# Which of several waits stands first: thirty places of an eight-layer kernel

## The reference

```python
x = x + spiking_attention(layernorm(x))   # 16 heads, q, k, v to spike means of 4 steps, softmax, projection
x = x + fp4_gated_ffn(layernorm(x))       # inputs and weights quantised in blocks of 16, silu(gate) * up, down
x = x + mamba4(layernorm(x))              # 4 layers; each: xz = x @ Wi.T; conv of 4 taps; u = silu(.);
                                          # dt = softplus(.); h_t = exp(dt_t*A)*h_(t-1) + dt_t*B_t*u_t;
                                          # y_t = C_t . h_t; (y + u*Dp) * silu(z) @ Wo.T
x = x + ternary_ffn(layernorm(x))
x = x + causal_linear_attention(layernorm(x))
x = x + top1_of_8_experts(layernorm(x))
x = x + long_convolution(layernorm(x))
x = x + dense_and_retrieved_experts(layernorm(x))   # top 8 of product keys, gathered up and down rows
```

## Time and profile before

| | |
|---|---|
| median of 3 runs | 1876.51 us (1872.69 to 1880.26) |
| profiled execution | 1873.34 us |
| its span | 1871.4 us, 27470 instructions |
| busy | PE 80%, PEld 57%, DVE 81%, ACT 71%, POOL 64% |
| granted TensorE clock, mean | 0.864 of full speed |
| DMA | 170.12 MB, mean 91 GB/s |

### The profile page before, as it was taken

One profiled execution on the slowest core, in us unless ns is written; L12 is line 12 of the kernel. 1 busy time (PEld: TensorE's weight loads), 2 busy tenths in 40 slices (PEclk: granted clock), 3 DMA queues, 4 the chain that ended last, 5 costly groups with the idle time before them and its releaser, 6 DMA issues.

```text
span 1871.4 us, 27470 instructions
## 1 busy us (share of the span) xinstructions
PE 1504.1 (80%) x9445; PEld 1072.7 (57%) x9445; DVE 1507.5 (81%) x2326; ACT 1324.6 (71%) x2672; POOL 1193.7 (64%) x999
## 2 busy tenths in 40 slices
PE   6777667567899988777788999878999887789976
PEld 3433334334577666544366776656666665667855
DVE  5688899999898799978998888898698998941254
ACT  4476656656897678777687877878688788754464
POOL 4158557666776568876765566878677778840046
PEclk7667777777999899878798999988799998899997
DMA  5032403423543433220343444331245542102300
GB/s 192 1 92 72 109 16 80 98 74 82 142 114 109 136 108 103 69 55 24 86 110 103 138 117 125 102 97 55 77 137 159 148 119 69 60 28 94 113 18 6
DMA packets 84586, 170.12 MB, mean 91 GB/s; under 512 B 9440, under 2 KB 14944, under 8 KB 84064
## 3 DMA queue, kind: packets, MB, share of 16 engines
q1 hardware_dynamic: 84448, 168.37, 32.7%
HBM read 99.13 MB, written 2.10 MB: 54 GB/s over the span
## 4 chain that ended last, share of the span: by engine, by line
PE 23%; DVE 16%; ACT 9%; POOL 7%; issue 5%; DMA 2%; SPq 1%; DVEq 0%; POOLq 0%; ACTq 0%
DVE m L1050 6%; DVE dtuB L1042 4%; PE ps L1473 3%; PE ps L1465 3%; ACT m L1026 3%; PE ps L1312 2%; PE ps L1180 2%; POOL o L1658 2%; POOL o L1653 2%; PE ps L965 2%; POOL m L1059 1%; PE ps L1756 1%; PE ps L1078 1%; ACT L347 1%; PE ps L1323 1%
## 5 line engine op out<-in xcount | busy, mean ns | idle before, releaser
L1059 POOL TENSOR_TENSOR m<-m 128x1024 f32<-128x1024 f32 x256 | 767.3, 3002 | 170.3 <-DVE m L1050 169.8
L1050 DVE TENSOR_TENSOR_SCAN m<-m,dtuB 128x1024 f32<-128x1024 f32 x256 | 584.4, 2283 | 31.5 <-PE ps L1078 10.0
L1026 ACT ACTIVATE m<-m,Aneg 128x255 f32<-128x255 f32 x1024 | 429.4, 496 | 26.7 <-DMA m<-m 18.5
L1042 DVE TENSOR_TENSOR dtuB<-m 128x1024 f32<-128x1024 f32 x256 | 374.7, 1464 | 13.1 <-DMA m<-m 6.2
L1465 PE MATMUL ps<-o 128*128 128x256 f32 x512 | 150.7, 406 | 19.8 <-DVE X L1409 11.8
L364 POOL TENSOR_TENSOR o<-o,mhalf 128x2 f32<-128x2 f32 x64 | 19.4, 304 | 222.2 <-DVE o L358 222.0
L1078 PE MATMUL ps<-m,w_const 128*32 128x256 f32 x2048 | 150.4, 425 | 7.4 <-POOL m L1059 7.3
L1432 ACT ACTIVATE o<-ps,w_mo 128x256 f32<-128x256 f32 x256 | 114.1, 472 | 59.7 <-PE ps L1465 58.0
L965 PE MATMUL ps<-m,wc 128*128 128x256 f32 x512 | 130.2, 411 | 10.9 <-ACT m L385 10.7
L1180 PE MATMUL ps<-o 128*128 128x256 f32 x512 | 127.2, 398 | 9.7 <-DVE o L1117 4.3
L1473 PE MATMUL ps<-o 128*128 128x128 f32 x1024 | 130.7, 281 | 3.2 <-ACT o L1432 3.1
(11 more groups left out here) (253 smaller groups left out, 2932.4 us busy)
## 6 DMA issues: line engine op xcount, KB each, us to landing
m<-m SPq DMA_DIRECT2D x256, 256.0 KB, 4.8
m<-spread SPq DMA_DIRECT2D x64, 512.0 KB, 4.9
o<-in_mox SPq DMA_DIRECT2D x128, 256.0 KB, 3.1
o<-in_l1x SPq DMA_DIRECT2D x88, 256.0 KB, 2.9
w_mb<-in_mb SPq DMA_DIRECT2D x1, 2290.0 KB, 12.1
m<-in_cwr SPq DMA_DIRECT2D x1, 2048.0 KB, 16.0
w_l3f<-in_l3f SPq DMA_DIRECT2D x1, 1536.0 KB, 17.6
X<-in_x SPq DMA_DIRECT2D x4, 256.0 KB, 6.6
```

The lines of the kernel that those rows point to most:

```text
L1026: op = e.activation(dA[at % NA][:, j, 1:CH], R[q][:, h * CH + 1:h * CH + CH], ACT.Exp, scale=Aneg[:, l, 4 * g + j:4 * g + j + 1])
L1042: e.tensor_tensor(dtuB[:, :, :], bc(R[q][:, (2 + h) * CH:(3 + h) * CH].unsqueeze(1), 4, CH), Br[k % 2], ALU.mult).then_inc(S.dve, n.tick(f ...
L1050: e.tensor_tensor_scan(flat(G[at % NG]), flat(dA[at % NA]), flat(dtuB[:, :, :]), 0.0, ALU.mult, ALU.add).then_inc(S.dve, n.tick(f"s{g}"))
L1059: e.tensor_tensor(G[at % NG], G[at % NG], Cr[k % 2], ALU.mult).then_inc(S.pool, n.tick(f"c{g}"))
```

## The change

The operations, their order on every engine and the set of waits ahead of each stay as they are (one exception of form: waits that stood ahead of a loop now stand ahead of its first instruction). In thirty places, over all stages, the waits ahead of an instruction are written in another sequence, so that another one stands first. The core of the diff; the places left out are of the same form (L0Attn, L0Ffn, L2Attn, L2Ffn, L3Attn and L3Ffn, most with a wait for a one-time load or a set-up value):

```diff
@@ -658,17 +658,17 @@
                 yield
+                e.wait_ge(T.pe, n.pe("qk"))
                 e.wait_ge(loaded["l0a"], 16)
-                e.wait_ge(T.pe, n.pe("qk"))
                 for i, name in enumerate(("q", "k")):
...
                 for h in range(16):
+                    e.wait_ge(T.pe, n.pe(f"s{h}"))
                     if h >= 4:
                         e.wait_ge(T.pe, n.pe(f"z{h // 4 - 1}{h % 4}"))
-                    e.wait_ge(T.pe, n.pe(f"s{h}"))
                     table(e, "exp")
@@ -683,8 +683,8 @@
                 yield
+                e.wait_ge(T.act, n.act("xT"))
                 e.wait_ge(loaded["l0a"], 16)
-                e.wait_ge(T.act, n.act("xT"))
                 for i, name in enumerate(("q", "k")):
@@ -696,8 +696,8 @@
                 def values(j):
+                    e.wait_ge(T.act, n.act(f"e{4 * j + 3}"))
                     e.wait_ge(T.pool, n.pool("vz3"))
-                    e.wait_ge(T.act, n.act(f"e{4 * j + 3}"))
                     for kt in range(2):
@@ -708,10 +708,10 @@
                     j, g = divmod(h, 4)
+                    if g == 0:
+                        e.wait_ge(T.dve, n.dve(f"m{j}"))
                     if h >= len(score):
                         e.wait_ge(T.act, n.act(f"e{h - len(score)}"))
-                    if g == 0:
-                        e.wait_ge(T.dve, n.dve(f"m{j}"))
                     for kt in range(2):
@@ -937,12 +937,13 @@
                 v, b = chains[k % 2], F.bank
+                if k >= 2:
+                    e.wait_ge(F.dve, n.dve("y"))
                 if k:
...
                     c, l = UNITS[k - 2]
-                    e.wait_ge(F.dve, n.dve("y"))
                     for i in range(2):
@@ -1016,11 +1017,11 @@
                     at, q, h = 8 * k + g, g % 4, g // 4
+                    if h == 0:
+                        e.wait_ge(*self.landed(n, q, 0))
                     if at >= NA:
...
                         e.wait_ge(S.dve, S.at(job, "dve", f"s{was}"))
-                    if h == 0:
-                        e.wait_ge(*self.landed(n, q, 0))
                     for j in range(4):
@@ -1028,34 +1029,36 @@
             def dve(self, e, n, k):
-                e.wait_ge(*self.spread(k, "B"))
-                if k == 0:
-                    e.wait_ge(U.pool, U.at(0, "pool", f"wc{NL - 1}"))
-                    for T in Os:
-                        e.wait_ge(T.act, T.at(0, "act", "e15"))
                 for g in range(8):
...
                         e.wait_ge(S.dve, n.dve(f"s{g - 1}") if g else S.at(k - 1, "dve", "s7"))
+                    if g == 0:
+                        e.wait_ge(*self.spread(k, "B"))
+                    if at == 0:
+                        e.wait_ge(U.pool, U.at(0, "pool", f"wc{NL - 1}"))
+                        for T in Os:
+                            e.wait_ge(T.act, T.at(0, "act", "e15"))
                     if h == 0:
...
                     yield
+                    e.wait_ge(S.dve, n.dve(f"b{g}"))
+                    e.wait_ge(S.act, n.act(f"a{g}"))
                     if at >= NG:
...
                         e.wait_ge(S.pe, S.at(job, "pe", f"y{was}"))
-                    e.wait_ge(S.act, n.act(f"a{g}"))
-                    e.wait_ge(S.dve, n.dve(f"b{g}"))
                     e.tensor_tensor_scan(flat(G[at % NG]), flat(dA[at % NA]), flat(dtuB[:, :, :]), 0.0, ALU.mult, ALU.add).then_inc(
...
             def pool(self, e, n, k):
-                e.wait_ge(*self.spread(k, "C"))
                 for g in range(8):
...
                     e.wait_ge(S.dve, n.dve(f"s{g}"))
+                    if g == 0:
+                        e.wait_ge(*self.spread(k, "C"))
                     e.tensor_tensor(G[at % NG], G[at % NG], Cr[k % 2], ALU.mult).then_inc(S.pool, n.tick(f"c{g}"))
@@ -1398,13 +1401,13 @@
                 yield
+                e.wait_ge(T.pe, n.pe("b2"))
                 e.wait_ge(T.act, n.act("xn1"))
-                e.wait_ge(T.pe, n.pe("b2"))
                 e.tensor_tensor(X2(c), ps2(self.bank(3)), X2(c), ALU.add).then_inc(T.dve, n.tick("b2"))
...
                 for x in range(8):
+                    e.wait_ge(T.pe, n.pe(f"y{x}"))
                     e.wait_ge(T.dve, n.dve(f"x{x - 1}1" if x else "b2"))
-                    e.wait_ge(T.pe, n.pe(f"y{x}"))
                     for i in range(2):
@@ -1426,9 +1429,9 @@
                     for k in range(4):
+                        e.wait_ge(T.pe, n.pe(f"h{x}{k}"))
                         if k == 0 and x >= 2:
                             e.wait_ge(T.pe, n.pe(f"y{x - 2}"))
-                        e.wait_ge(T.pe, n.pe(f"h{x}{k}"))
                         e.activation(v.hd[x % 2][:, k, :], self.bank(5 * x + 4 + k)[:, 0:CH], ACT.Relu,
@@ -1465,10 +1468,11 @@
                         yield
-                    e.wait_ge(*self.landed(n, 2 * x + 1))
                     for k in range(4):
...
                             e.wait_ge(T.act, n.act(f"h{x}{max(k, 2)}"))
+                        if k == 0:
+                            e.wait_ge(*self.landed(n, 2 * x + 1))
                         for i in range(2):
@@ -1610,11 +1614,15 @@
                     yield
-                    e.wait_ge(T.pe, n.pe(f"D{i}"))
                     for h in range(4):
-                        e.wait_ge(T.pool, n.pool(f"E{i}{h}"))
+                        if h % 2 == 0:
+                            e.wait_ge(T.pool, n.pool(f"E{i}{h}"))
                         if i or h:
                             e.wait_ge(T.pool, n.pool(f"w{i}{h - 1}" if h else f"w{i - 1}3"))
+                        if h % 2:
+                            e.wait_ge(T.pool, n.pool(f"E{i}{h}"))
+                        if h == 0:
+                            e.wait_ge(T.pe, n.pe(f"D{i}"))
                         e.scalar_tensor_tensor(v.md, v.Em[h % 2], v.s8[:, h, 7:8], o[:, :], ALU.is_ge, ALU.mult).then_inc(
@@ -1641,8 +1649,8 @@
                             e.tensor_tensor(v.e64, v.e64, bc(v.rinv.unsqueeze(2), 4, 64), ALU.mult).then_inc(T.pool, n.tick(f"r{i}"))
+                            e.wait_ge(T.pool, n.pool(f"r{i}"))
                             e.wait_ge(T.dve, n.dve(f"fl{i}"))
-                            e.wait_ge(T.pool, n.pool(f"r{i}"))
                             p4 = v.e64.rearrange("p h (a b) -> p (h a) b", b=8)
```

More of the change, by code:

```diff
@@ L645, in pool @@
                 yield
+                e.wait_ge(T.act, n.act("xn1"))
                 e.wait_ge(loaded["l0a"], 16)
-                e.wait_ge(T.act, n.act("xn1"))
                 e.tensor_tensor(X2(c), X2(c), row(w("l0a", "ob")), ALU.add).then_inc(T.pool, n.tick("ob"))
                 yield
+                e.wait_ge(T.dve, n.dve("u3"))
                 e.wait_ge(U.pool, U.at(0, "pool", T.name))
-                e.wait_ge(T.dve, n.dve("u3"))
                 spread_pool(e, n, T, v.va)
@@ L1316, in values @@
                 def values(j):
+                    e.wait_ge(T.act, n.act(f"p{2 * j + 1}"))
                     e.wait_ge(T.pool, n.pool("vz3"))
-                    e.wait_ge(T.act, n.act(f"p{2 * j + 1}"))
                     for i in range(2):
@@ L1384, in dve @@
                 yield from norm_dve(e, n, T, v, X2(c))
+                e.wait_ge(T.pe, n.pe("lg"))
                 e.wait_ge(loaded["mo"], 16)
                 e.wait_ge(loaded["const"], 16)
-                e.wait_ge(T.pe, n.pe("lg"))
                 e.tensor_tensor(v.lg, self.bank(1)[:, 0:16].rearrange("p (a b) -> p a b", a=2), bc(w("mo", "gb").unsqueeze(1), 2, 8),
@@ L1491, in dve @@
                 yield from norm_dve(e, n, T, v, X2(c))
+                e.wait_ge(T.act, n.act("xT"))
                 e.wait_ge(loaded["l3a"], 16)
                 e.wait_ge(U.dve, U.at(0, "dve", "r7"))
-                e.wait_ge(T.act, n.act("xT"))
                 e.tensor_tensor(v.xa, v.xT, Apow[:, :], ALU.mult).then_inc(T.dve, n.tick("xa"))
+                e.wait_ge(T.dve, n.dve("xa"))
                 e.wait_ge(U.pool, U.at(0, "pool", "onesF"))
-                e.wait_ge(T.dve, n.dve("xa"))
                 e.tensor_tensor_scan(v.sc, bc(onesF[:, 0:1], CH), v.xa, 0.0, ALU.mult, ALU.add).then_inc(T.dve, n.tick("s0"))
@@ L1504, in dve @@
                 yield
+                e.wait_ge(T.pe, n.pe("o"))
                 e.wait_ge(T.pool, n.pool("pb"))
-                e.wait_ge(T.pe, n.pe("o"))
                 e.tensor_tensor(v.r, ps2(T.banks[1]), v.xn, ALU.add).then_inc(T.dve, n.tick("r"))
@@ L1544, in pe @@
                 yield
+                e.wait_ge(T.act, n.act("gl"))
                 e.wait_ge(loaded["l3a"], 16)
-                e.wait_ge(T.act, n.act("gl"))
                 for i in range(2):
@@ L1749, in pe @@
                         yield
-                    e.wait_ge(T.dve, n.dve(f"x{i - 1}" if i else "d"))
                     for h in range(4):
                         e.wait_ge(T.act, n.act(f"w{i}{h}"))
+                        if h == 0:
+                            e.wait_ge(T.dve, n.dve(f"x{i - 1}" if i else "d"))
```

## The result

| | before | after |
|---|---|---|
| median of the runs, us | 1878.38 (1872.69 to 1881.46, 4 runs) | 1850.82 (1848.11 to 1857.45, 4 runs) |
| ratio, 95% interval | | 0.9862 (0.9824 to 0.9900) |
| profiled execution, us | 1873.34 | 1852.99 |
| its span, us, and granted clock | 1871.4, 0.864 | 1851.2, 0.863 |

The forecast was 1856.5 us, with a range from 1842 to 1873 and 0.74 on faster; the sum made for the profiled execution was 1853.3. So the total was right. The experiments show that its parts were not. The medians are 27.6 us apart; the ratio, which is one of means, makes it 26.

The account below looks back on a forecast made before the run. It held that no engine is saturated and hand-overs between instructions cost visible time. Latencies of 8 us and hand-overs between jobs of 12 took 1873.3 to 1853.3 us; the median, 3.2 above, was 1856.5, range 1842 to 1873.

Parts of the forecast that it names:

- What bounds it: Whole kernel: no engine saturated (DVE 81%, PE 80% busy); hand-overs a visible part, issue 97 us of the chain.
- The scan, 0.10 us a place: Scan L1050: its product's wait moves onto the instruction, saving 0.10 us at 27 chain pieces, 2.7 us from 681 us on.
- Other separate waits and PE, (1.9 + 1) x 1.57: Other late waits moved onto instructions: 31 chain pieces at 0.06 us save 1.9 us, PE's 1; scaled to the whole run.
- 0.6 x 1.57 against for the wrong-way ones: L716 and L673 now carry an early wait, the late one separate: 0.6 us lost on the chain, scaled by 1.57.
- The hand-over: Between scan jobs, DVE's product starts before POOL's at 11 places: 2.2 us less each on DVE, 1.04 more on POOL.
- take half of 24: Of DVE's 24 us saved at hand-overs between jobs, half reaches the end: 12 us, bounds 0 and 24.
- The sum, 8 + 12: Whole kernel: 8 us from wait latencies plus 12 from hand-overs, 1873.3 to 1853.3 us for the profiled execution.
- Only the latencies: Rival: L1042 shortens, but its gain becomes waiting for landings, or POOL still begins first; 1868.5 us, chance 0.22.
- POOL becomes the bound: Rival: POOL's longer last product delays L1078, L843 and the front; up to 24 us more, 1900 us, chance 0.04.
- The place of a wait costs nothing: Rival: the 0.12 us before the scan are DVE's own finish; time stays 1876.5 us, chance 0.04.
- Signs: Profile after: product-to-scan gap 0.04 us without wait piece, L1042 mean about 1370 ns, L1059 about 3047, issue under 90 us.

Follow-up runs that it names:

- e7: Changed kernel with L716's wrong-way waits turned back and six kinds of late separate wait written first: 1853.2 us, ratio to before 0.9848.
- e5: Kernel before with one satisfied wait written first at POOL's product of group 7, so POOL starts later: 1855.5 us, ratio 0.9884.
- e6: Changed kernel with a satisfied wait written first at group 4 of DVE's product ahead of the scan: 1891.7 us, ratio to before 1.0058.
- the place: The edit of DVE's product ahead of the scan: at group 0 the wait for the last scan rides on it; alone on the kernel before, 1850.1 us.
- e1: Changed kernel with B's landing written first again at group 0 of the product ahead of the scan: 1869.0 us, ratio to before 0.9933.
- e2: Kernel before with only the waits of the product ahead of the scan (L1042) in the new order: 1850.1 us, ratio 0.9846.
- e12: Changed kernel with POOL's product waiting for DVE's next product (groups 0 to 6) instead of the scan: 1855.2 us, ratio to before 0.9866.
- e3: Kernel before with only the scan's three waits (L1050) turned round: 1871.9 us, ratio 0.9956.
- e4: Kernel before with all of the change except the scan and the product ahead of it (28 places): 1869.9 us, ratio 0.9937.
- e8: Kernel before with both DVE edits of the scan stage, product and scan, and none of the other 28: 1852.5 us, ratio 0.9866.
- e11: Kernel before with only the edit of the product ahead of the scan, measured again: 1849.1 us, ratio 0.9849.

## Why the prediction was right, point by point

The total is right with some luck: the mechanism holds, the sizes of its two terms do not, as the sum shows.

*What bounds it:* right. No engine was saturated, and hand-overs were what there was to gain.

*The scan, 0.10 us a place:* the size of the latency is right (132 to 35 ns). As a term it was 2.7 x 1.57 = 4 us; alone it measures 8 (4 to 12), and on top of the product's edit nothing that can be told.

*Other separate waits and PE, (1.9 + 1) x 1.57, and 0.6 x 1.57 against for the wrong-way ones:* alone 12 us (7 to 17) where 4 were taken; on top of the product's edit, again nothing that can be told. e7, which turns back the wrong-way waits of L716, cannot tell their cost from nothing; those of L673 no run took alone.

*The hand-over:* the mechanism, its eleven places, 2.2 and 1.04 us, and the mean of 1370 ns (measured 1365) and of 3047 (3046) are right; e5 and e6 show it as the cause. The step that failed is "take half of 24". Alone the place gives 28 or 29 us, all of DVE's 23 and more. On top of the other edits it gives 13 to 18, and there half of 24 is near.

*The sum, 8 + 12:* the profiled pair is 20 us apart too (1873.34 and 1852.99), but that is chance: the profiled execution of before was 5 us under the median of its runs. The runs give 26 to 30. The sum came near because two errors met: the hand-over was put at less than half of what it gives alone, and the latencies were added to it although the terms do not add. With the terms as measured alone the sum would have been 49. Taken the other way about, the other edits first, it is 13 and then 13 to 18, both above the 8 and 12 of the forecast.

*Rivals.* "Only the latencies" gave 1868.5 us, and the kernel that has only the latencies (e1) measures 1869.0; it fell since the place was worth its price. "POOL becomes the bound" fell: with 11 us more of POOL the kernel is faster (e2, e5), and 26 less (e6) and 160 less (e12) brought no gain, though neither of these two changes POOL's time alone. "The place of a wait costs nothing" fell by e3 and e4.

*Signs:* 0.03 us from product to scan (0.04 predicted), group 0 without long products, the two means as above, issue down by 14 us on the chain from 700 us on (91 to 77), where 97 to under 90 was asked from 681 us on. DVE's separate wait ahead of the scan did not vanish from the chain: it is a piece nine times, six of them behind 681 us where there were 27; it now holds ACT's and PE's waits.

What stays open is why the place alone gives more than the busy time it takes from DVE. Over the 59 runs of before, time and PE's mean granted clock go together (correlation -0.72; 1867.8 us at 0.864, 1890.0 at 0.854), and every kernel with the place had a mean clock of 0.864 to 0.871 against 0.859. By that line of 12 us per 0.01 some 6 to 14 us of the gain go with the clock. Among the kernels with the place the order is another: e8 has the highest mean clock (0.871 over its runs) and is no faster than e11 (0.866). Whether the clock makes the time or follows it was not tested.

## What to carry to other kernels

Where the same event releases two instructions that slow each other, here products on DVE and POOL with all inputs in SBUF, look at who starts first, to 10 ns: here 12 ns decided 2.2 us, and the engine that the chain hangs on must be the one whose late wait rides on its instruction. Elsewhere write the late wait first as well, but do not sum its 0.06 to 0.10 us over the program: here they could no longer be told once one larger edit was in. And judge by medians of several runs: one profiled execution was up to 7 us off within its first 193 us.

## What the runs showed of the hardware

- *A wait's price by its place.* From the end of the releasing scan to the start, at the hand-overs: DVE 35 ns when the late wait rides on the instruction, 91 when it is in a separate one; POOL 79 to 80 and 145. So a separate late wait costs 56 ns on DVE and 65 on POOL at this place, 97 ns at the scan (132 to 35, from the product's end), and 0.06 us on PE. The Trainium skill's 50 to 100 ns for reading a semaphore ("Advanced Engine Details and Errata", section "Network/Comms") fits all four. POOL starts 45 to 54 ns later than DVE on the same event with the same form of wait; that head start is what makes the edit work.
- *The exclusion is not even.* The product of DVE that starts second takes 3.4 us instead of 1.23, POOL's that starts second 3.4 instead of 2.35; in both cases the two together end about 3.44 us after the first start, 0.14 us less than their lengths alone add up to (1.23 + 2.35). The scan, which reads one input from SBUF and one from PSUM, runs beside POOL's product with no change of length: its mean is 2283 ns before, after and in e12, where POOL's product lies beside it much more.
- *A satisfied wait can be worth 22 us.* e5's only edit is one more wait instruction on POOL, 32 times; by it POOL starts second at eleven places.
